# Stack transfers head by head with a semaphore for each, and new order tables, in a kernel of four attention layers

## What is computed

```python
def _L3_conv_ref(hidden_states, gn_gamma, gn_beta, wq, bq, wk, bk, wv, bv, wo, bo, ln_gamma, ln_beta):
    x = _group_norm(hidden_states, gn_gamma, gn_beta)
    x = x.reshape(B, C, H * W).transpose(0, 2, 1)
    q = x @ wq.T + bq
    k = x @ wk.T + bk
    v = x @ wv.T + bv
    ...
    scores = jnp.einsum('bhid,bhjd->bhij', q * scale, k)
    probs = jax.nn.softmax(scores.astype(jnp.float32), axis=-1).astype(scores.dtype)
    ctx = jnp.einsum('bhij,bhjd->bhid', probs, v)
    ctx = ctx.transpose(0, 2, 1, 3).reshape(B, T, C)
    out = _layer_norm(ctx @ wo.T + bo, ln_gamma, ln_beta)
    out = out.transpose(0, 2, 1).reshape(B, C, H, W)
    return (out + residual) / RESCALE
```

## Time and profile before

| what | value |
|---|---|
| median of 3 runs | 2812.36 us (2811.44 to 2816.11) |
| span of the profiled execution | 2818.8 us |
| PE busy | 2605.2 us, 92% of the span |
| DVE busy | 1864.0 us, 66% |
| ACT busy | 1291.2 us, 46% |
| POOL busy | 597.3 us, 21% |
| mean granted clock of TensorE | 0.928 of full speed |
| stage "fronts" | 0 to about 470 us |
| six stages "both" | about 470 to 2470 us, 331 to 334 us each once they repeat |
| stage "backs" | from about 2470 us to the end |

### The profile page before, as it was taken

How to read it: one execution, slowest core, us unless ns; L and a number is a source line. 1 busy time by engine, 2 the same in 40 slices (tenths; PEclk the granted TensorE clock), 3 DMA queues, 4 the chain that set the end, 5 groups by cost and what they waited for, 6 DMA issues and landing times.

```text
span 2818.8 us, 26455 instructions
## 1 busy us (share of the span) xinstructions
PE 2605.2 (92%) x9892; PEld 1429.7 (51%) x9892; DVE 1864.0 (66%) x1925; ACT 1291.2 (46%) x2209; POOL 597.3 (21%) x322
## 2 busy tenths in 40 slices
PE   7979988989999999999999999998999999978887
PEld 4556653464644646454564645546464455643332
DVE  4544227687477765777666875868656876568985
ACT  3353221646345462555526454364624546135466
POOL 0083120050110501023020401105010040224473
...
GB/s 88 1 0 1 1 30 16 9 37 1 75 1 45 1 8 68 1 45 1 49 27 1 45 1 75 1 30 16 1 75 1 45 1 16 45 45 46 46 1 30
DMA packets 29297, 72.15 MB, mean 26 GB/s; under 512 B 10224, under 2 KB 10416, under 8 KB 28912
## 3 DMA queue, kind: packets, MB, share of 16 engines
...
## 4 chain that ended last, share of the span: by engine, by line
PE 70%; DVE 17%; ACT 4%; SPq 4%; issue 3%; POOL 2%; DMA 1%; DVEq 0%; ACTq 0%; POOLq 0%
PE ps L632 11%; PE ps L665 11%; PE ps L651 9%; PE ps L783 8%; PE ps L952 7%; PE ps L874 6%; PE ps L640 4%; PE ps L787 4%; DVE ba_nmx L1328 4%; SPq L496 3%; DVE fa_nmx L1328 2%; PE ps L721 2%; PE ps L860 2%; DVE accb L1496 2%; DVE xm L1381 1%
## 5 line engine op out<-in xcount | busy, mean ns | idle before, releaser
L1181 ACT ACTIVATE prb<-ps 128x512 f32<-128x512 f32 x896 | 493.5, 603 | 318.2 <-PE ps L665 294.6
L1328 DVE TENSOR_REDUCE ba_nmx<-ps 128x1 f32<-128x1024 f32 x448 | 529.0, 1218 | 129.4 <-PE ps L651 129.3
L1496 DVE TENSOR_TENSOR accb<-accb,prb 128x1024 f32<-128x1024 f32 x312 | 385.4, 1263 | 90.2 <-ACT prb L1181 89.0
L665 PE MATMUL ps<-qs,ks 97*128 97x512 f32 x896 | 366.1, 484 | 37.2 <-DMA qs<-ba_nmx_r 28.1
L1042 ACT ACTIVATE pr<-ps 128x512 f32<-128x512 f32 x336 | 195.9, 596 | 360.0 <-PE ps L874 271.9
L651 PE MATMUL ps<-ks,qs 96*128 96x512 f32 x896 | 330.2, 475 | 26.5 <-DVE ba_nmx L1328 15.9
L554 POOL TENSOR_TENSOR q2k<-pr,q2k 128x512 fp32r<-128x512 f32 x112 | 145.8, 1318 | 845.6 <-ACT q2k L1079 845.6
L665 PEld LDWEIGHTS ps<-qs,ks 97*128 97x128 f32 x896 | 165.9, 203 | 286.0 <-ACT prb L1181 179.5
L952 PE MATMUL ps<-prb,vb 128*32 128x512 f32 x1792 | 249.5, 630 | 2.6 <-ACT prb L1181 2.5
L651 PEld LDWEIGHTS ps<-ks,qs 96*128 96x128 f32 x896 | 174.9, 210 | 145.9 <-DVE ba_nmx L1328 75.0
L1328 DVE TENSOR_REDUCE fa_nmx<-ps 128x1 f32<-128x1024 f32 x168 | 198.1, 1216 | 47.6 <-PE ps L860 37.1
...
## 6 DMA issues: line engine op xcount, KB each, us to landing
...
qs<-ba_nmx_r SPq DMA_DIRECT2D x56, 4.0 KB, 1.8
```

The costliest lines, as they stand in the source:

```text
L665: return pe.matmul(o.ps[:, bank, :], keys[0:ROW + 1, tile(jt)], queries[0:ROW + 1, cols(ic)], start=True, stop=True)
L1181: act.activation(weights3(o, s, g), o.ps[:, turn3[score_use(s, g) % 3], :], ACT.Exp)\
L1328: dve.tensor_reduce(o.nmx[:, head, it:it + 1], o.ps[:, bank:bank + 2, :], AX.XY, ALU.max, negate=True).then_inc(o.max_sb[n].sem, 1)
L1496: dve.tensor_tensor(o.sums[pair], o.pairs[(s - 1) % 2][pair] if j == 1 else o.sums[pair], o.pairs[s % 2][pair], ALU.add).then_inc(done.sem, 1)
```

## The change

Three things are done. First, `stacks` waits for all four planes of `part`, and then sends the six transfers of head 0, those of head 1, and so on. Second, the semaphores are now one for each head g (`o.stacked[g]`), counted through both units: the first tile of each head waits for its own six transfers, and the helper `part_taken` makes ACT wait for all four heads. Third, every table of `ORDER` has new numbers, so that instructions of every engine stand in another order against each other; their number is unchanged. Lines behind the tables move by one to seven.

```diff
@@ -75,59 +75,60 @@
 ORDER = {
     ("fronts", "PE"): (
-        0, 1, 2, 2, 3, 1, 6, 1, 1, 2, 2, 1, 1, 1, 2, 1, 4, 1, 3, 1, 4, 1, 2, 1, 1, 1, 1, 2, 1, 2, 1, 1, 2, 2, 1,
...
+        2, 3, 4, 1, 5, 1, 1, 1, 2, 2, 4, 1, 1, 1, 1, 1, 5, 1, 2, 1, 2, 1, 2, 2, 1, 2, 1, 1, 1, 1, 1, 2, 1, 3,
...
@@ -358,7 +359,7 @@
-            o.stacked = [alone(f"stacked{u}", 16 * 6 * QUAD)[3] for u in range(CH)]
+            o.stacked = [alone(f"stacked{g}", 16 * 6 * CH)[3] for g in range(QUAD)]
@@ -485,17 +486,17 @@
                 def stacks(b, u):
                     if u:
                         sp.wait_ge(o.scored[3].sem, o.scored[3].at(b, QUAD * STEPS3))
-                    for done, src, dst, rows in ((o.q_hi, 0, o.queries, (0, 2)), (o.q_lo, 1, o.queries, (1,)),
-                                                 (o.k_hi, 2, o.keys, (0, 1)), (o.k_lo, 3, o.keys, (2,))):
+                    for done, src in ((o.q_hi, 0), (o.q_lo, 1), (o.k_hi, 2), (o.k_lo, 3)):
                         sp.wait_ge(done[3].sem, done[3].at(b, IC * (u + 1)))
-                        if src == u == 0 and b == o.turns[0]:
-                            row = o.keys[ROW:ROW + 1, :, :].rearrange("p g (n c) -> p (g n) c", c=P)
-                            sp.dma_start(bf32(row), ones[0:QUAD * NT, :]).then_inc(o.ones.sem, 16)
-                        for r in rows:
-                            for g in range(QUAD):
+                    if u == 0 and b == o.turns[0]:
+                        row = o.keys[ROW:ROW + 1, :, :].rearrange("p g (n c) -> p (g n) c", c=P)
+                        sp.dma_start(bf32(row), ones[0:QUAD * NT, :]).then_inc(o.ones.sem, 16)
+                    for g in range(QUAD):
+                        for dst, rows in ((o.queries, (0, 1, 0)), (o.keys, (2, 2, 3))):
+                            for r, src in enumerate(rows):
                                 sp.dma_start(bf32(dst[L * r:L * r + L, g, :]),
-                                             bf32(part[L * g:L * g + L, src, :])).then_inc(o.stacked[u].sem, 16)
-                            yield
+                                             bf32(part[L * g:L * g + L, src, :])).then_inc(o.stacked[g].sem, 16)
+                        yield
@@ -900,9 +901,10 @@
                     def maxima(u):
-                        pe.wait_ge(o.stacked[u].sem, o.stacked[u].at(b, 16 * 6 * QUAD))
                         for k in range(QUAD * NT):
                             g, it = divmod(k, NT)
+                            if it == 0:
+                                pe.wait_ge(o.stacked[g].sem, o.stacked[g].at(b, 16 * 6 * (u + 1)))
@@ -1009,6 +1011,11 @@
+            def part_taken(o, b, u):
+
+                for g in range(QUAD):
+                    act.wait_ge(o.stacked[g].sem, o.stacked[g].at(b, 16 * 6 * (u + 1)))
@@ -1189,7 +1196,7 @@
-                        act.wait_ge(backs[0].stacked[0].sem, backs[0].stacked[0].at(B - 2, 16 * 6 * QUAD))
+                        part_taken(backs[0], B - 2, 0)
@@ -1199,11 +1206,11 @@
-                            act.wait_ge(o.stacked[0].sem, o.stacked[0].at(b, 16 * 6 * QUAD))
+                            part_taken(o, b, 0)
                             if b == B - 2:
-                                act.wait_ge(backs[1].stacked[0].sem, backs[1].stacked[0].at(B - 1, 16 * 6 * QUAD))
+                                part_taken(backs[1], B - 1, 0)
                             if b == B - 1:
-                                act.wait_ge(backs[0].stacked[1].sem, backs[0].stacked[1].at(B - 2, 16 * 6 * QUAD))
+                                part_taken(backs[0], B - 2, 1)
```

32 lines of the change are left out of this document (16 added, 16 removed), and 45 rows, old and new, of the table ORDER.

## The result

| | before | changed |
|---|---|---|
| median of the runs | 2814.08 us (2811.44 to 2816.11, 4 runs) | 2776.09 us (2775.06 to 2779.41, 4 runs) |
| span of the profiled execution | 2818.8 us | 2773.5 us |
| mean granted clock of TensorE | 0.928 | 0.941 |

What follows compares the result with a forecast made beforehand. PE was taken to bound the stages both, DVE the stage backs. Terms -7, -36 and -16 give -59 us on the 2818.8 us span, 2760; less 6.4 us of span above the median, 2753 us, range 2724 to 2792.

Steps and rivals of the forecast that it cites:

- The serial start, -7: Image 0's first maxima, with no other work beside them: head 0 lands at 421.6 instead of 428.9, -7 us.
- the stacks give PE nothing in themselves: Six stages both: PE has other work before the maxima, so earlier transfers only change what fills PE; the order tables count.
- The stages, -6 each: Six stages both: DMA wait -2.75, turn -2, clock -1 and -1, wait at normalisation +1; -36 us in all.
- the clock, -1 and -1: Stage both: less time at low clock behind the turn, -1 us, and at layer 0's maxima, -1 us.
- Rival 2: Clock comes back after the maxima's DMA wait and at layer 0's maxima: about -11 us a stage, 2724 us; chance 0.16.
- The stage "backs", -16: Last stage: second units' maxima start sooner after the other lane's scores, -16 us, bounds -8 and -20.
- 20 remain among them, 8 x 1.18 = 9.4 us less: T = 2514.0 + 46.8: Stage backs, `ba`'s first 64 scores: 20 maxima among them instead of 28, so 46.8 us instead of 56.2.
- From there to the end order and counts are nearly the same: Stage backs, after `bb`'s second maxima start: nothing changes to the end, so the 16 us gained stay.
- the eleven maxima ahead of it cover it: Stage backs, `ba`'s first score: the whole stack lands 4.4 us later, hidden by eleven maxima ahead of it.
- Rival 1: Gaps in stages both only move elsewhere, stages stay: 2789 us, chance 0.20; at its worst 2812 us, chance 0.04.
- Rival 3: Runs of maxima behind layer 1's hold the clock down 23 us more a stage: +69 us, 2822 us; chance 0.05.
- Rival 4: A head's six transfers land only with all 24, ten places wait 11.4 us more: 2867 us; chance 0.02.

Runs made afterwards that it cites:

- e4_old_tables: The kernel before with transfers and semaphores by head, all order tables as before (SP's adapted to four steps a unit): 2820.66 us, ratio 1.0016 to the kernel before.
- e7_pool_small: The changed kernel with 24 of POOL's 28 additions per image in the stage backs cut to one column of each half, leaving work out: 2728.88 us.
- e1_old_backs: The changed kernel with all engines' order tables of the stage backs put back to those of before (SP's adapted): 2769.81 us.
- e9_dve_adds: The changed kernel with POOL's 56 additions in the stage backs moved to DVE, nothing left out: 2767.18 us.
- e12_fill_early_dve: e9_dve_adds plus q high's transfers sent early in first units and unread filler matmuls at two places of each stage both: 2760.04 us.
- e11_pieces: The changed kernel with two pieces of layer 1's weighing put back ahead of the second unit's last maximum in PE's stage both table: 2791.04 us.

## Why the prediction was right, and where not

- **The serial start, -7: right.** e4_old_tables, which has the old order, shows -6.8, with the first maximum 21.3 us behind the group norm (28.0 before). The changed kernel's other 4 us come from the new order of the fronts, ahead of all transfers (the group norm 4.7 us earlier). I had costed that table at nothing without saying so.
- **The stages, "the stacks give PE nothing in themselves": right** for the old order (0.4 us a stage). With the new one I should have said that they must be early: without it a stage loses 17 us.
- **The stages, -6 each: mis-sized, 8.4.** The wait for the maxima's DMA: -2.0 in the trace for my -2.75, and its undo cost 2.5. The turn: -2.8 for my -2. The wait at the normalisation: +0.1 for my +1. What I undersized is above all the clock, -1 and -1. Two places of low clock went entirely, and PE's busy time fell by 5.9 us in the pair of stages shown, where I had 2 for both. Idle time fell by 3.5 there, 1.2 less than these waits add up to, as small new ones came up. Rival 2 had the mechanism and one of the places, layer 0's maxima. At the DMA's wait, its dearer place, the clock did not come back: 2.7 us of waiting are still enough to lose it. It came back at the turn instead.
- **The stage "backs", -16: wrong, +15.** The failed step is "20 remain among them, 8 x 1.18 = 9.4 us less: T = 2514.0 + 46.8". It takes `ba`'s scores to be bounded by DVE alone, and DVE's time to be a sum over instructions. Neither holds. In the earlier trace rows PE is busy for 51.3 of the 55 us, nearly as full as DVE; with DVE relieved in e7_pool_small the stretch still takes 54.8. And of the 52.5 us that I read as DVE's work a part was DVE standing behind POOL. The stretch came out at 65.5 us, 18.7 above my 46.8: 10.7 of these go when POOL's additions are cut short, 8.0 stay. Five maxima left the stretch where I had eight, and the additions grew in it (2.28 us each but for a head's first, 1.96 before). The rest of the loss is idle time: PE and DVE waited on each other in turn, and PE ran at 0.84 of its clock. Why the new order makes them wait isn't shown.
- **Behind it: a second wrong step.** "From there to the end order and counts are nearly the same" puts the last stretch at nothing; it lost 10.5 us. Over the whole stage DVE is busy for 12.9 us more with the same instructions, 9.4 of them in the normalisation and the layer norm. By their length more of them ran beside POOL's additions (2.8 us each at the longest, 0.7 alone). No kernel with POOL's additions cut in the old order was run, so how much of the stage's 14.9 us is this stays open. That 7.1 of them are the new order's and 7.8 the transfers' is shown by e1_old_backs.
- **`ba`'s first score: 7.1 us later, I had 4.4.** In the new order it stands behind PE's own eleven maxima and the projections among them: the early transfers bring it from 39.9 us behind the group norm (e9_dve_adds) to 38.3 (e12_fill_early_dve) and no further. In the old order they bring it from 39.0 to 33.9. So "the eleven maxima ahead of it cover it" fails: in the new order PE's own line sets when the first score comes, and with the stack early that is still later than the 37.2 us that I had with the stack late. The steps on the transfers were right: each second unit's maxima came 5.5 to 6.5 us behind the scores.
- **The rivals.** Rival 1 falls with e11_pieces. Rival 3 didn't occur: behind layer 1's maxima PE is at the low level for 14 us as before. Rival 4 falls with the first maximum, 6.0 us behind the first issue of image 0's transfers.
- **The sum.** -59 against -45.3: 4 us and 15 us more than forecast in the first two parts, 32 less in the third. The range held in part by luck, because the first two errors made up for more than half of the third. That is 13.7 of the 23 us that the forecast misses. The other 9 are the last step, "I take that off too": the profiled execution of the kernel before was 6.4 us above its median, that of the changed kernel 2.6 us below its own.
